# Attention block: causal mask products ahead of the score products in the second block's banks

## The chip, the cores and the metric

The kernel runs on one core of a Trainium2 chip. The metric is the device time of one execution in microseconds; the time before is 558.08 us, the median of three runs (558.05 to 559.54).

## The reference, cut to what matters

Sixteen sequences of 256 tokens, width 128, go through layer norm and causal attention with 16 heads (query and key width 8, value width 64), then through layer norm and a mixture of 8 experts. The change is in the causal scores:

```python
scores = jnp.einsum('bhqd,bhkd->bhqk', q, k) / scale
causal = jnp.triu(jnp.ones((T, T), dtype=bool), k=1)
scores = jnp.where(causal, -jnp.inf, scores)
attn = jax.nn.softmax(scores, axis=-1)
```

## The kernel before, in words

The work of the attention is cut into 64 units (`UNITS = B * G`): one sequence of 16, and one group of 4 heads of 16. The 256 queries of a unit are two blocks. Queries 0 to 127 see keys 0 to 127 only; their scores for 4 heads fill one PSUM bank, `s0_ps` (128 queries x 4 heads x 128 keys). Queries 128 to 255 see all 256 keys; their scores fill two banks, `s1_ps` (128 queries x 4 heads x 256 keys), heads 0 and 1 in the first bank, heads 2 and 3 in the second. In the trace both tiles are called `s_ps`.

The heads are packed so that one matmul does several. A unit's queries `qT` have 32 rows for each head, and `k_diag` holds the keys of head i in the rows of head i and zeros elsewhere. The scores of the first block are one matmul over all 128 rows (line 1276, 512 columns). Those of the second block are two matmuls over 64 rows each (line 1189): rows 0 to 63 (heads 0, 1) write the first bank, rows 64 to 127 (heads 2, 3) the second. The two use different halves of TensorE's array, so they run side by side.

The causal mask is added by matmuls too. In the second block only keys 128 to 255 need one. It goes in two halves of 64 keys, each for both row halves: four matmuls (line 1194) of a 64 x 128 stationary `half_rows` and a moving `half_masks` of 64 columns, broadcast over two heads (128 columns), all bf16. The operands of line 1189 are of type fp32r (shown as f32 in rows), and each of the two writes all 512 columns of its bank; it begins the sum there (`start=True`), and the masks are added.

```python
tiles = ((slice(0, HALF), 0), (slice(HALF, P), 2))
for rows, i in tiles:
    nc.tensor.matmul(s1_ps[:, i:i + 2, :], qT[kb][rows, q, P:T], k_diag[kb][rows, q, i:i + 2, :], start=True, stop=False, ...)
```

Every matmul of the program is a weight load (LDWEIGHTS, the engine PEld in rows) and a product (MATMUL, PE in rows).

Each engine's order is written out by hand, in a function `batch` for each engine: 20 batches of 4 units, some of them in a hardware loop. In step u TensorE does, in this order: scores and masks of the second block of unit u+1 (the block that the change touches, behind a wait on `exp1`, the count of units whose second block ScalarE has finished reading), eight transposes of the probabilities of unit u-1 (`turn`, lines 1048 and 1049), in one of four steps each the products of the query and key projection, a router product or transposes of a norm, the context of unit u-2 (`contexts`, line 1075), the output projection of unit u-3 (`project`, line 1084), four more transposes (`turn_last`, line 1058), a part of the value projection for a later unit (lines 1034 to 1036), and the first block's scores of unit u+2 (line 1276), behind a wait on `filled0`.

VectorE takes the row maximum of the first block (line 939, after `s0_done`) and of the second (line 883, after `s1_done`), and refills `s0_ps` with the mask (line 892). ScalarE takes the exponentials (line 529), 4 for each block. GpSimd scales the probabilities (lines 482 and 489). The increment of `s1_done` stands on the last matmul of the block that is changed. After unit 63 the experts follow, on TensorE's matmuls too.

Of the kernel before, what the change touches and what calls it, by code (L numbers as in the profile page):

```python
# [13 lines left out]
P = 128  # L14
B, T, D = 16, 256, 128
# [27 lines left out]
def has(index, n):  # L43

    return not isinstance(index, int) or 0 <= index < n


def await_count(engine, sem, count):

    if not isinstance(count, int) or count > 0:  # L50
        engine.wait_ge(sem, count)


def bcast(ap, axis, n):

    ap = ap.unsqueeze(axis)
    shape = list(ap.shape)
    shape[axis] = n
    return ap.broadcast_to(shape)
# [6 lines left out]
def block_kernel(nc, x, w_q, w_k, w_v, w_o, gate_w, w1, w2, out):  # L66
# [3 lines left out]
    with ExitStack() as ctx:  # L70
# [3 lines left out]
        def ps(name, shape):  # L74
            return ctx.enter_context(nc.psum_tensor(name, shape, F32))
# [47 lines left out]
        with ExitStack() as early:  # L123
            def sa(name, shape, dt=F32):
                return sb(name, shape, dt, early)

            k_diag_even = sa("k_diag_even", [P, G, HG, T], F32R)
            k_diag = [k_diag_even, sa("k_diag_odd", [P, G, HG, T], F32R)]
            qT = [sa(f"qT{r}", [P, G, T], F32R) for r in range(RING)]
# [14 lines left out]
            half_rows = sa("half_rows", [P, 2, P], BF16)  # L144
            half_masks = sa("half_masks", [P, 2, HALF], BF16)
# [29 lines left out]
        s1_ps = ps("s1_ps", [P, HG, T])  # L175
# [854 lines left out]
        def _(pe):  # L1030
            pe.wait_ge(consts2, 3)

            def split_product(out_, w_h, w_l, x_h, x_l):
                nc.tensor.matmul(out_, w_h, x_h, start=True, stop=False)  # L1034
                nc.tensor.matmul(out_, w_h, x_l, start=False, stop=False)  # L1035
                return nc.tensor.matmul(out_, w_l, x_h, start=False, stop=True)  # L1036
# [141 lines left out]
            def batch(b, par):  # L1178
                for j in range(G):
                    u = b * G + j  # L1180
                    r1, r2, rm = (j + 1) % RING, j % RING, (j + 1) % RING
                    if has(u + 1, UNITS):
                        q, kb = (j + 1) % G, par if j < 3 else 1 - par
                        if isinstance(u, int) and u == -1:
                            pe.wait_ge(halves, 10)
                        await_count(pe, exp1, u + 1)
                        tiles = ((slice(0, HALF), 0), (slice(HALF, P), 2))
                        for rows, i in tiles:
                            nc.tensor.matmul(s1_ps[:, i:i + 2, :], qT[kb][rows, q, P:T], k_diag[kb][rows, q, i:i + 2, :],  # L1189
                                             start=True, stop=False, skip_group_check=True)  # L1190
                        for half in range(2):
                            cols = slice(P + half * HALF, P + (half + 1) * HALF)
                            for rows, i in tiles:
                                last = nc.tensor.matmul(s1_ps[:, i:i + 2, cols], half_rows[rows, half, :],  # L1194
                                                        bcast(half_masks[rows, half, :], 1, 2),
                                                        start=False, stop=(half == 1), skip_group_check=True)
                        last.then_inc(s1_done, 1)
                    if has(u - 1, UNITS):
                        turn(u - 1, rm)
                    if j == 3 and has(b + 2, B):  # L1200
# [5 lines left out]
                        for w in range(2):  # L1206
                            last = split_product(misc_ps[0][:, w * T:(w + 1) * T], wqk_hi[:, w, :], wqk_lo[:, w, :],
                                                 xT_hi[par][:, :], xT_lo[par][:, :])
# [12 lines left out]
                    if j == 2 and has(b + 2, B):  # L1221
                        pe.wait_ge(xn1_ready, b + 3)
                        await_count(pe, v_ready, u + 2)
                        for tb in range(TB):
                            last = nc.tensor.transpose(misc_ps[0][:, tb * P:(tb + 1) * P], xn1[:, tb, :], ident[:, :])
# [19 lines left out]
                    if has(u + 2, UNITS):  # L1245
                        w, q = u + 2, (j + 2) % G
# [16 lines left out]
                        cols = slice((q // 2) * 512, (q // 2 + 1) * 512)  # L1263
                        split_product(misc_ps[0][:, :], xT_hi[xb][:, toks], xT_lo[xb][:, toks],
                                      wv_hi[:, cols], wv_lo[:, cols]).then_inc(v_done, 1)
                    if has(u + 2, UNITS):

                        q, kb = (j + 2) % G, par if j < 2 else 1 - par
# [5 lines left out]
                        if isinstance(u, int) and u == -2:  # L1274
                            nc.tensor.matmul(s0_ps[:, :, :], ident_bf[:, :], bcast(causal[:, :], 1, HG), start=True, stop=True)
                        nc.tensor.matmul(s0_ps[:, :, :], qT[kb][:, q, 0:P], k_diag[kb][:, q, :, 0:P], start=False, stop=True,  # L1276
                                         skip_group_check=True).then_inc(s0_done, 1)

            batches(pe, batch)
            turn(63, 1)  # L1280
            gather(2)
# [92 lines left out]
```

## Time and profile before

| | us |
|---|---|
| median of three runs | 558.08 |
| the profiled execution's own time | 557.51 |
| its span, first to last instruction | 555.8 |
| TensorE (PE) busy in the span | 525.8 |
| VectorE busy | 416.0 |
| ScalarE busy | 405.1 |
| GpSimd busy | 253.6 |
| all 128 matmuls of line 1189 (mean 0.50 each) | 64 pairs |
| all 256 matmuls of line 1194 (median 0.226 each) | 64 times four |

A matmul's row gives its start and a duration that holds its load's rest, its columns and its way through the array; consecutive matmuls overlap, so that the rate at which TensorE works is read from the distance between starts, not from durations. A row "x2" or "x4" in the timeline is several instructions merged: the start of the first, and the time to the end of the last. "64*128 64x512" is a stationary of 64 rows by 128 columns and a moving operand of 64 rows by 512 columns.

### The profile page before, as it was taken

The numbers are of one execution on the slowest core, as the hardware profiler recorded it, in microseconds if no ns is written. First come the engines' busy times: TensorE is split into PE (matmuls) and PEld (weight loads), VectorE is DVE, ScalarE is ACT, GpSimd is POOL, SyncE is SP. The second block draws the span as 40 slices with busy tenths as digits, with TensorE's granted clock in tenths as the row PEclk, the third lists the DMA queues.
The fourth block names the chain that finished last, engine by engine and source line by source line (L and its number), as shares of the span: only waits on it lengthen the run. The fifth ranks groups of instructions, "written<-read, shape, count | busy, mean of one in ns | idle before, by whom it ended". The sixth has DMA issues, their size and how long they took to land.

```text
span 555.8 us, 13959 instructions
## 1 busy us (share of the span) xinstructions
PE 525.8 (95%) x4777; PEld 426.6 (77%) x4777; DVE 416.0 (75%) x1066; ACT 405.1 (73%) x1383; POOL 253.6 (46%) x249
## 2 busy tenths in 40 slices
PE   1489999999999999999999999999999999999996
PEld 1257777777777777778777777777689989999995
DVE  1477888888888888888898998899973876442354
ACT  4699989889888888889889898889655434334330
POOL 5165565565555655565464555457820111011011
PEclk9989999999999999999999999999999999999999
DMA  4577152731633325142250423501200011000011
GB/s 123 151 186 196 39 151 63 243 115 39 173 105 102 90 61 151 38 113 77 77 153 20 133 77 77 140 14 43 92 21 1 2 40 59 20 21 11 11 29 49
DMA packets 49783, 45.97 MB, mean 83 GB/s; under 512 B 4288, under 2 KB 46528, under 8 KB 49728
## 3 DMA queue, kind: packets, MB, share of 16 engines
q1 hardware_dynamic: 48864, 44.60, 29.2%
q8 instruction: 32, 0.52, 0.4%
q10 hardware_dynamic: 864, 0.66, 0.4%
q14 instruction: 23, 0.19, 0.1%
HBM read 26.35 MB, written 18.89 MB: 81 GB/s over the span
## 4 chain that ended last, share of the span: by engine, by line
PE 86%; DVE 5%; ACT 5%; DMA 2%; issue 2%; ACTq 0%; POOL 0%; DVEq 0%
PE ctx_ps L1075 15%; PE misc_ps L1084 11%; PE t_ps L1162 10%; PE t_ps L1048 6%; PE s_ps L1189 5%; PE t_ps L1049 5%; PE t_ps L1058 4%; PE misc_ps L1034 3%; PE s_ps L1146 3%; PE misc_ps L1036 3%; PE misc_ps L1035 3%; ACT prob L529 3%; PE s_ps L1276 2%; PE s_ps L1147 2%; PE s_ps L1148 2%; PE ctx_ps L1172 2%
## 5 line engine op out<-in xcount | busy, mean ns | idle before, releaser
L529 ACT ACTIVATE prob<-s_ps,neg_max 128x128 f32<-128x128 f32 (+1 forms) x512 | 209.6, 436 | 20.6 <-DVE neg_max L939 17.5
L489 POOL TENSOR_TENSOR probn<-prob,inv 128x1024 f32<-128x1024 f32 x64 | 121.2, 1893 | 55.3 <-DVE inv L960 55.3
L529 ACT ACTIVATION_READ_ACCUMULATOR prob<-s_ps,neg_max 128x1 f32 x512 | 113.6, 222 | 0.0
L482 POOL TENSOR_TENSOR probn<-prob,inv 128x512 f32<-128x512 f32 x64 | 66.5, 1040 | 74.6 <-PE t_ps L1058 66.8
L883 DVE TENSOR_REDUCE neg_max<-s_ps 128x4 f32<-128x1024 f32 x64 | 76.3, 1193 | 1.1 <-PE s_ps L1194 1.1
L1084 PE MATMUL misc_ps<-wo_sb,ctxT 128*128 128x128 f32 x512 | 73.9, 287 | 0.7 <-DVE x_all L708 0.7
L506 POOL TENSOR_TENSOR y_parts<-y_sb,y_parts 128x512 fp32r<-128x512 f32 x16 | 20.6, 1286 | 112.9 <-ACT y_parts L587 112.9
L1084 PEld LDWEIGHTS misc_ps<-wo_sb,ctxT 128*128 128x128 f32 x512 | 62.0, 191 | 11.4 <-issue 11.4
L577 ACT ACTIVATE hT<-s_ps 128x512 f32<-128x512 f32 x64 | 38.0, 596 | 44.7 <-PE s_ps L1148 42.2
L1048 PE MATMUL t_ps<-ident,probn 128*128 128x128 f32 x256 | 63.7, 289 | 0.8 <-ACT probT L543 0.7
L1049 PE MATMUL t_ps<-ident,probn 128*128 128x128 f32 x256 | 60.2, 275 | 0.0
L939 DVE TENSOR_REDUCE neg_max<-s_ps 128x4 f32<-128x512 f32 x64 | 44.2, 691 | 16.9 <-PE s_ps L1276 16.4
L753 DVE COPY probT<-t_ps 128x512 f32<-128x512 f32 x64 | 44.1, 689 | 15.7 <-PE t_ps L1058 15.1
L1075 PE MATMUL ctx_ps<-probT,v_odd 128*64 128x256 f32 (+1 forms) x512 | 48.7, 332 | 0.0
L1075 PE MATMUL ctx_ps<-probT,v_even 128*64 128x256 f32 (+1 forms) x512 | 48.7, 332 | 0.0
L747 DVE COPY ctxT<-ctx_ps 128x512 f32<-128x512 f32 x64 | 43.6, 682 | 0.7 <-PE ctx_ps L1075 0.4
L892 DVE CAST s_ps<-causal 128x512 f32<-128x512 bf16 x63 | 42.4, 672 | 0.0
L1075 PEld LDWEIGHTS ctx_ps<-probT,v_odd 128*64 128x64 f32 x512 | 31.7, 136 | 13.9 <-issue 3.6
L1048 PEld LDWEIGHTS t_ps<-ident,probn 128*128 128x128 f32 x256 | 36.1, 141 | 8.0 <-issue 1.3
L1075 PEld LDWEIGHTS ctx_ps<-probT,v_even 128*64 128x64 f32 x512 | 31.7, 136 | 13.6 <-issue 3.2
L543 ACT ACTIVATE probT<-t_ps 128x512 f32<-128x512 f32 x64 | 41.1, 642 | 0.0
L1146 PE MATMUL s_ps<-xin_hi,w_hi 128*128 128x256 f32 x128 | 38.7, 302 | 0.6 <-issue 0.2
(176 smaller groups left out, 1155.2 us busy)
## 6 DMA issues: line engine op xcount, KB each, us to landing
qT<-q_rows SPq DMA_DIRECT2D x15, 512.0 KB, 4.0
q_rows<-qk_hi SPq DMA_DIRECT2D x32, 128.0 KB, 2.4
q_rows<-qk_lo SPq DMA_DIRECT2D x32, 128.0 KB, 2.4
k_diag_odd<-k_rows SPq DMA_DIRECT2D x32, 128.0 KB, 4.2
k_rows<-qk_hi SPq DMA_DIRECT2D x30, 128.0 KB, 2.4
k_rows<-qk_lo SPq DMA_DIRECT2D x30, 128.0 KB, 2.4
k_diag_even<-k_rows SPq DMA_DIRECT2D x28, 128.0 KB, 4.2
w_raw<-in_L_ffn_w SPq DMA_DIRECT2D x1, 2048.0 KB, 9.3
```

What stands on the lines that cost most here:

```text
L482: nc.gpsimd.tensor_tensor(probn[r][:, 0:HG * P].rearrange("p (i k) -> p i k", i=HG), prob[r][:, 0:HG * P].rearrange("p (i k) -> p i k", i=HG),
L489: nc.gpsimd.tensor_tensor(probn[r][:, HG * P:].rearrange("p (i k) -> p i k", i=HG), prob[r][:, HG * P:].rearrange("p (i k) -> p i k", i=HG ...
L529: last = nc.scalar.activation(prob[r][:, first + i * keys:first + (i + 1) * keys], scores[:, i, :], ACT.Exp, bias=neg_max[:, r, block_, i: ...
L753: nc.vector.tensor_copy(probT[rm][:, 1024:1536], t_ps[rm][:, :]).then_inc(t_dve, 1)
L883: nc.vector.tensor_reduce(out=neg_max[:, r1, 1, :], in_=s1_ps[:, :, :], axis=AX.X, op=ALU.max, negate=True).then_inc(max1, 1)
L939: nc.vector.tensor_reduce(out=neg_max[:, r2, 0, :], in_=s0_ps[:, :, :], axis=AX.X, op=ALU.max, negate=True).then_inc(max0, 1)
L1048: nc.tensor.transpose(t[:, i, 0:P], q0[:, 2 * f + i, :], ident[:, :])
L1049: last = nc.tensor.transpose(t[:, i, P:T], q1[:, 2 * f + i, 0:P], ident[:, :])
L1075: last = nc.tensor.matmul(ctx_ps[half * DV:(half + 1) * DV, pair, kb * P:T], v_sb[vb][:, kb, h * DV:(h + 1) * DV], rhs, start=(kb == 0), s ...
L1084: last = nc.tensor.matmul(misc_ps[1][:, tb * D:(tb + 1) * D], ctxT[r][:, c, tb * P:(tb + 1) * P], wo_sb[:, 2 * g + c, :], start=(g == 0 an ...
L1146: nc.tensor.matmul(to, w1_hi[:, e, at_], xh, start=True, stop=False)
L1162: last = nc.tensor.matmul(y_ps[half * CAP:(half + 1) * CAP, q, :], hT[m % RING][:, half, c, q * CAP:(q + 1) * CAP], w2_of(2 * (m % EP) + h ...
```

## The change

The four mask products of the second block go first, and the two score products behind them. The first mask product in each bank carries `start=True`; all the others, the scores among them, add to what is there, or write where nothing of this sum has been written yet. The increment of `s1_done` moves from the last mask product to the second score product. The wait on `exp1` stays ahead of the first of the six. No instruction is added or taken away.

```diff
                         tiles = ((slice(0, HALF), 0), (slice(HALF, P), 2))
-                        for rows, i in tiles:
-                            nc.tensor.matmul(s1_ps[:, i:i + 2, :], qT[kb][rows, q, P:T], k_diag[kb][rows, q, i:i + 2, :],
-                                             start=True, stop=False, skip_group_check=True)
                         for half in range(2):
                             cols = slice(P + half * HALF, P + (half + 1) * HALF)
                             for rows, i in tiles:
-                                last = nc.tensor.matmul(s1_ps[:, i:i + 2, cols], half_rows[rows, half, :],
-                                                        bcast(half_masks[rows, half, :], 1, 2),
-                                                        start=False, stop=(half == 1), skip_group_check=True)
+                                nc.tensor.matmul(s1_ps[:, i:i + 2, cols], half_rows[rows, half, :],
+                                                 bcast(half_masks[rows, half, :], 1, 2),
+                                                 start=(half == 0), stop=False, skip_group_check=True)
+                        for rows, i in tiles:
+                            last = nc.tensor.matmul(s1_ps[:, i:i + 2, :], qT[kb][rows, q, P:T], k_diag[kb][rows, q, i:i + 2, :],
+                                                    start=False, stop=True, skip_group_check=True)
                         last.then_inc(s1_done, 1)
```

TensorE's order in a unit of the steady part, between the first block's scores and the transposes (`k_diag_odd` is the key tile of one of two sequences in flight, `probn` the scaled probabilities):

```order
 L1276 MATMUL s_ps<-k_diag_odd,qT 128x512 [waits filled0]
-L1189 MATMUL s_ps<-k_diag_odd,qT 128x512 [waits exp1]
-L1189 MATMUL s_ps<-k_diag_odd,qT 128x512
-L1194 MATMUL s_ps<-half_masks,half_rows 128x2x64 x4
+L1191 MATMUL s_ps<-half_masks,half_rows 128x2x64 [waits exp1]
+L1191 MATMUL s_ps<-half_masks,half_rows 128x2x64 x3
+L1195 MATMUL s_ps<-k_diag_odd,qT 128x512 x2
 L1048 MATMUL t_ps<-ident,probn 128x128 [waits t_act,normed]
 L1049 MATMUL t_ps<-ident,probn 128x128
```

The wait on `exp1` now stands on the first mask product; what comes ahead of the six and behind them is the same. The first unit of all, at the program's start, where the scores of the first block follow on a bf16 product (line 1275), and the query and key projection follows:

```order
 L1275 MATMUL s_ps<-causal,ident_bf 128x512 [waits first_loaded]
 L1276 MATMUL s_ps<-k_diag_even,qT 128x512
-L1189 MATMUL s_ps<-k_diag_even,qT 128x512 [waits halves]
-L1189 MATMUL s_ps<-k_diag_even,qT 128x512
-L1194 MATMUL s_ps<-half_masks,half_rows 128x2x64 x4
+L1191 MATMUL s_ps<-half_masks,half_rows 128x2x64 [waits halves]
+L1191 MATMUL s_ps<-half_masks,half_rows 128x2x64 x3
+L1195 MATMUL s_ps<-k_diag_even,qT 128x512 x2
 L1034 MATMUL misc_ps<-xT_hi,wqk_hi 128x256 [waits v_ready,xT_ready]
```

The wait on `halves` (the mask constants) moved with the first of the six. The orders of the other engines are the same before and after.

## Rows read from the trace of the kernel before

**Rows 1.** The page, part 1: busy time of each engine
```profile
PE 525.8 (95%) x4777; PEld 426.6 (77%) x4777; DVE 416.0 (75%) x1066; ACT 405.1 (73%) x1383; POOL 253.6 (46%) x249
```
**Rows 2.** Busy time, three stretches: us, then PE, PEld, DVE, ACT, POOL, clock, DMA
```profile
42.60:366.20 323.60, 323.54 (x2732) 251.60 (x2732) 279.75 (x704) 286.95 (x1094) 184.50 (x163) 1.00 0.38 104
366.20:398.00 31.80, 30.40 (x260) 23.60 (x260) 30.14 (x76) 28.48 (x99) 22.13 (x17) 1.00 0.19 59
398.00:555.80 157.80, 151.32 (x1688) 137.94 (x1686) 85.33 (x234) 60.18 (x105) 28.25 (x25) 1.00 0.08 23
```
**Rows 3.** Chain that ended last, in order of time, where it enters and leaves TensorE
```profile
40.78 1.83 ACT prob L529 x8
42.62 0.04 issue
42.66 0.50 PE s_ps L1189
...
366.25 1.48 PE ctx_ps L1075 x16
367.73 0.04 issue
```
**Rows 4.** Line 1189 from 42.6 to 365: count, ns min/median/max, idle before
```profile
L1189 PE MATMUL s_ps<-k_diag_odd,qT x56: 491/500/504, 42.7 to 341.2; 64*128 64x512 f32 x56
L1189 PE MATMUL s_ps<-k_diag_even,qT x56: 491/500/501, 65.5 to 364.6; 64*128 64x512 f32 x56
  ACT prob L529: 0.9, 2
```
**Rows 5.** Timeline of PE in one unit: start us, us, instruction
```profile
204.36 0.60 PE L1058 MATMUL t_ps<-ident,probn 128*128 128x128 f32 x4
204.72 0.48 PE L1034 MATMUL misc_ps<-wv_hi,xT_hi 128*128 128x512 f32 x1
205.03 0.39 PE L1035 MATMUL misc_ps<-wv_lo,xT_hi 128*128 128x512 f32 x1
205.26 0.39 PE L1036 MATMUL misc_ps<-wv_hi,xT_lo 128*128 128x512 f32 x1
205.50 0.40 PE L1276 MATMUL s_ps<-k_diag_even,qT 128*128 128x512 f32 x1
205.82 0.50 PE L1189 MATMUL s_ps<-k_diag_even,qT 64*128 64x512 f32 x2
206.17 0.29 PE L1194 MATMUL s_ps<-half_masks,half_rows 64*128 64x128 bf16 x4
206.38 0.33 PE L1048 MATMUL t_ps<-ident,probn 128*128 128x128 f32 x1
```
**Rows 6.** The same, windows begun late: the last of line 1058, the last two of line 1194
```profile
204.69 0.27 PE L1058 MATMUL t_ps<-ident,probn 128*128 128x128 f32 x1
206.23 0.22 PE L1194 MATMUL s_ps<-half_masks,half_rows 64*128 64x128 bf16 x2
```
**Rows 7.** Timeline of the weight loads (PEld) in the same unit
```profile
205.04 0.19 PEld L1036 LDWEIGHTS misc_ps<-wv_hi,xT_lo 128*128 128x128 f32 x1
205.82 0.19 PEld L1189 LDWEIGHTS s_ps<-k_diag_even,qT 64*128 64x128 f32 x2 [0.36 <-issue]
206.16 0.12 PEld L1194 LDWEIGHTS s_ps<-half_masks,half_rows 64*128 64x128 bf16 x4 [0.16 <-issue]
```
**Rows 8.** Timeline of PE and PEld at the first unit, clock at half
```profile
22.68 0.65 PE L1275 MATMUL s_ps<-causal,ident_bf 128*128 128x512 bf16 x1
22.77 0.98 PE L1276 MATMUL s_ps<-k_diag_even,qT 128*128 128x512 f32 x1
22.68 0.36 PEld L1276 LDWEIGHTS s_ps<-k_diag_even,qT 128*128 128x128 f32 x1
```
**Rows 9.** Timeline of ACT and DVE around the same unit as rows 5
```profile
204.85 0.26 ACT L529 ACTIVATION_READ_ACCUMULATOR prob<-s_ps,neg_max 128x1 f32 x1
205.93 0.69 DVE L939 TENSOR_REDUCE neg_max<-s_ps 128x4 f32<-128x512 f32 x1 [0.24 <-PE s_ps L1276]
206.62 1.19 DVE L883 TENSOR_REDUCE neg_max<-s_ps 128x4 f32<-128x1024 f32 x1
204.95 0.66 ACT L543 ACTIVATE probT<-t_ps 128x512 f32<-128x512 f32 x1
```

## Prediction

> **What bounds the kernel now.** I read the page's busy times first: TensorE is busy for 525.8 us of the 555.8 us span, every other engine for 75% or less [rows 1]. By stage this is sharper. From 42.6 to 366.2 us, the steady part of the attention, TensorE is busy 323.54 of 323.60 us at full granted clock, with VectorE at 279.75 and ScalarE at 286.95 [rows 2]. The chain that ended last says the same: it enters TensorE at 42.66 us with a product of line 1189, and runs on that engine alone until the context products that begin at 366.25 us [rows 3]. From there to 398 us the chain goes through VectorE and ScalarE (30.14 and 28.48 us busy of 31.80), and from 398 us on TensorE leads again [rows 2]. So in the steady part what shortens TensorE's stream shortens the kernel, one for one, and what shortens it after 366 us does not, or in part.
>
> The block of six matmuls that is reordered stands 64 times in the program. In the steady part line 1189 has 56 + 56 matmuls, two to a block, so 56 blocks [rows 4].
>
> Then the timeline of TensorE within one unit, by distances between starts [rows 5, 6]:
> - scores, line 1189, start at 205.82; masks, line 1194, at 206.17: 0.35 us
> - first pair of masks at 206.17, second pair at 206.23: 0.06 us
> - second pair of masks at 206.23, transposes, line 1048, at 206.38: 0.15 us
>
> The block takes 206.38 - 205.82 = 0.56 us. The same three distances stand in all the steady blocks that I looked at, to 0.01 us.
>
> What makes up the 0.35 us? Two products of 512 columns that follow each other in full height (all 128 rows) start 205.50 - 205.26 = 0.24 us apart (0.23 for the two before) [rows 5]. There the next weight load starts 0.01 us after the product ahead of it and is done in its shadow (205.04 against 205.03) [rows 5, 7]. At line 1189 the load and the product start together, at 205.82: the array had just changed from one tile of 128 rows to two of 64, and nothing hides this load [rows 5, 7]. So 0.35 - 0.23 = 0.12 us of the block is a bare load of fp32r weights. The last transpose of line 1058 gives 0.11: it starts at 204.69, line 1034 needs a load of the same size behind it, and line 1035 starts at 205.03, 0.34 later, which is 0.11 for the load and 0.23 for the product [rows 5, 6]. Starts are rounded to 0.01, so I split the 0.41 us from the scores to the second masks as 0.34 + 0.07 (it reads 0.35 + 0.06); the whole block, 0.56, stays.
>
> **The change, part by part.** Nothing is added or removed; the six matmuls and their six loads stay. Their order changes what each load can hide behind.
>
> 1. *Change into the 64-row tiles.* Line 1276 to the block: 205.82 - 205.50 = 0.32 us [rows 5]. It is 0.09 more than 0.23, the array running empty. It is still there, now ahead of a mask product. Taken as unchanged: 0.
>
> 2. *First to second pair of masks.* 0.07 us, taken over from the split above. The first pair's own load was as bare before as it is now: in the old order the mask loads too started only at 206.16, when the scores' columns were through [rows 7].
>
> 3. *Second pair of masks to the scores.* This pair of kinds (bf16, 128 columns, then an fp32r load on the same 64 rows) is not in the trace. The near row is line 1058 to line 1034, 128 columns and then an fp32r load in full height: the load takes 0.11 us from the start of the product ahead, the product's 0.05 us of columns lie inside it [rows 5, 6]. Bounds: from below 0.06 us, if the load were wholly hidden (then the masks' own columns set it); from above 0.17 us, if the load starts when the columns are through (0.06 + 0.11). I take 0.11. For it speaks also the first unit of all: there the fp32r load of line 1276 starts in the same hundredth as the bf16 product of line 1275 (22.68 us), and line 1276 is there 0.09 us later, long before the 0.65 us of that product are over [rows 8]. So a bf16 product does not keep back an fp32r load behind it.
>
> 4. *Scores to the transposes.* Now the 512 columns stand last in the 64-row tiles, with a change back to full height behind them. The same in the other direction is line 1276 to line 1189, 0.32 us [rows 5]. The other way to it: masks to transposes take 0.15 now for 0.05 of columns, so 0.10 for the change of tiles; 0.10 + 0.23 = 0.33. I take 0.32 to 0.33.
>
> The new block: 0.07 + 0.11 + 0.33 = 0.51 us. The old one: 0.56 us. **Gain 0.05 us for each block**, 56 x 0.05 = 2.8 us.
>
> In words: 0.11 us of bare load at the front are traded for a load that is half hidden by the second pair of masks.
>
> The eight blocks outside: the first four (23 to 38 us) stand where ScalarE or the clock sets the pace, the last four where the chain is VectorE's and ScalarE's [rows 2, 3]. I cost them at nothing; all eight at the full rate would be 0.4 us.
>
> *Waits.* The wait on `exp1` stands ahead of the six as before. Behind it on TensorE stands everything else, so I looked at how far it is from holding: ScalarE's last step on the unit before ends at 204.85 + 0.26 = 205.11, and the block starts at 205.82, 0.71 us later [rows 5, 9]. In the whole steady part ScalarE held this line for 0.9 us, twice, at the very start [rows 4]. The transposes of line 1048 wait for ScalarE's copy, which ends at 204.95 + 0.66 = 205.61 against 206.38: 0.77 us to spare [rows 5, 9]. A block shorter by 0.05 us uses up none of this, since each unit's ScalarE work begins with a TensorE product that now comes earlier by as much. VectorE needs 279.75 us for what would take 320.8 instead of 323.6, ScalarE 286.95 [rows 2]. *The increment of `s1_done`* is now on the second score product. It would come some 0.05 us earlier than before; and VectorE's line 883 starts at 206.62, when its own line 939 is over, not when the increment comes [rows 9]. Worth nothing, and costs nothing.
>
> *SP's and GpSimd's queues* issue in the same order; the loads of `qT` and `k_diag` wait on `s1_done` of a sequence before, and that moves with the rest.
>
> Sum against the profiled execution: 557.51 - 2.8 = 554.7 us. The median of the runs shown is 0.57 us above this execution: 558.08 - 2.8 = **555.3 us**, 0.5% less than before. About 0.3% (1.7 us) is what a measurement of this kernel can tell from no change.
>
> **A rule weighed against it.** The four mask loads of a block lie within 0.12 us, and the second pair's products start 0.06 us after the first's [rows 5 to 7], so a load on 64 rows can lie under a product on the same 64 rows. But the mask loads behind the scores did not: they start 0.34 us after them [rows 7]. The Trainium skill (TensorE: Matmul & The Clock Gate, Part 3) says that a weight load overlaps with products in flight only when their row groups differ. By that rule the scores' load would wait out the second masks. The skill's Part 2 allows a load into a background weight buffer as well, which is what the mask rows look like. The rule as a mechanism is the first rival.
>
> **The rivals.**
> - *The load waits for the masks' columns: no difference.* Step 3 is 0.17 instead of 0.11 us: the block is 0.07 + 0.17 + 0.33 = 0.57 against 0.56, the time 558.1 (with half a hundredth either way, 557.8 to 558.4). For it: between line 1189 and line 1194, the only change of kind inside the 64-row tiles, the load was not hidden [rows 7]. Against it: the load behind line 1275 was, and the second mask loads are [rows 7, 8]. Chance 0.20.
> - *Slower: a bf16 product on 64 rows must drain before an fp32r load on the same rows begins*, as at a change of tiles. Place: between the second masks and the scores, in every unit. Price: 0.15 (masks to what follows a drain) + 0.11 (bare load) = 0.26 in step 3, the block 0.07 + 0.26 + 0.33 = 0.66, 0.10 longer; 56 x 0.10 = 5.6 us, 563.7 us. It decides from step 3 above 0.16 us, where the gain is gone. For it only that the load behind line 1189 was late; against it that it was late by no more than the columns, and not by a drain. Chance 0.05.
> - *More than forecast.* The scores' load is hidden wholly (step 3 = 0.06), or the change of tiles behind fp32r costs less than I took. The block is 0.46 us, the gain 56 x 0.10 = 5.6 us, 552.5 us. For it nothing in the rows but the loads that are grouped tightly; against it that one load at a time lies ahead of the running product everywhere else. Chance 0.06.
> - *TensorE's gain is lost to a wait on ScalarE or VectorE:* it needs the 0.7 us to spare to go; it counts to the no-difference case, with 0.02 of its own.
>
> **How the numbers follow.** Forecast 0.67, no difference 0.20 + 0.02, slower 0.05, more 0.06. The forecast's own range is a gain of 0.035 to 0.07 us a block (steps 3 and 4 each off by a hundredth or so), 2.0 to 3.9 us, 554.2 to 556.1 us. The range must also take in no difference: 554.0 to 558.4 us; outside it stand the slower case, the large gain and a little of each side. Faster by over 0.3% (below 556.4): 0.67 + 0.06 = 0.73. Slower: 0.05. Within: 0.22.
>
> **What would show each step right or wrong.** In the timeline of the changed kernel: masks first, the second pair 0.07 us after the first; the scores' load starts with the second pair and not 0.05 us behind it; the transposes start 0.51 us after the first mask (0.57: no difference; 0.66: slower). Units of the steady part lie 0.05 us closer, and the context products at which the chain leaves TensorE begin at about 363.5 us instead of 366.25 us. The forecast is wrong if the start of the transposes is 0.55 us or more behind the first mask, or if waits for ScalarE appear ahead of the masks.

## The result and the profile after

The changed kernel takes 555.28 us (median of 4 runs, 554.97 to 555.69), the kernel before 558.28 us (the three runs shown ahead and one more). The ratio is 0.9945, 95% interval 0.9933 to 0.9957: 3.0 us less. In a later series on one chip the changed kernel took 554.18 us against 558.23 us, ratio 0.9931 (0.9909 to 0.9954). Forecast were 555.3 us and a gain of 2.8 us.

The profiled execution took 555.17 us, with a span of 553.4 us. First the page's part 1, which answers to [rows 1]:

```profile
PE 524.4 (95%) x4777; PEld 424.7 (77%) x4777; DVE 415.9 (75%) x1066; ACT 405.9 (73%) x1383; POOL 253.9 (46%) x249
```

The same stretches as [rows 2], in the changed kernel's times (us, then PE, PEld, DVE, ACT, POOL, clock, DMA):

```profile
43.30:363.96 320.66, 320.63 (x2730) 249.31 (x2730) 279.37 (x704) 287.32 (x1092) 184.52 (x163) 1.00 0.38 104
363.96:396.00 32.04, 30.45 (x260) 23.55 (x260) 30.35 (x76) 28.61 (x100) 22.28 (x17) 1.00 0.18 59
396.00:553.40 157.40, 151.09 (x1687) 137.73 (x1685) 85.19 (x234) 60.22 (x105) 28.19 (x25) 0.99 0.08 23
```

The steady part is still all TensorE's, and it is 320.66 us long where it was 323.60: the gain is in the stage where it was looked for. The two stages behind it kept their lengths to 0.4 us, and the start, ahead of it, is 0.70 us longer.

TensorE's busy time over the whole span fell by only 1.4 us (525.8 to 524.4), and a reader who had only that would miss half of the gain. In the steady part it fell by 2.91 us (323.54 to 320.63). Ahead of it, it rose by 1.7 us, and there the two profiled executions differ in the granted clock, 0.96 before and 0.88 after:

```profile
0.00:42.60 42.60, 20.55 (x103) 13.44 (x103) 20.79 (x55) 29.47 (x89) 18.73 (x46) 0.96 0.58 156
0.00:43.30 43.30, 22.26 (x103) 14.09 (x103) 21.03 (x55) 29.72 (x89) 18.88 (x46) 0.88 0.63 167
```

The chain that ended last, where it enters and leaves TensorE, as in [rows 3] (start us, us, what):

```profile
41.44 1.83 ACT prob L529 x8
43.28 0.05 issue
43.32 0.28 PE s_ps L1191 x4
...
364.05 1.48 PE ctx_ps L1075 x16
365.53 0.04 issue
```

It enters 0.66 us later than before and leaves 2.20 us earlier. The later entry is no effect of the order: in a second profile of the same code (below), with a granted clock of 0.96 in the start, the unit that starts here at 49.51 us starts at 48.62 us, and before it started at 48.87 us.

The timeline of PE in the same unit as [rows 5], and the second pair of masks from a window begun late, as in [rows 6]:

```profile
204.48 0.39 PE L1036 MATMUL misc_ps<-wv_hi,xT_lo 128*128 128x512 f32 x1
204.71 0.40 PE L1276 MATMUL s_ps<-k_diag_even,qT 128*128 128x512 f32 x1
205.04 0.28 PE L1191 MATMUL s_ps<-half_masks,half_rows 64*128 64x128 bf16 x4
205.14 0.48 PE L1195 MATMUL s_ps<-k_diag_even,qT 64*128 64x512 f32 x2
205.55 0.33 PE L1048 MATMUL t_ps<-ident,probn 128*128 128x128 f32 x1
...
205.11 0.22 PE L1191 MATMUL s_ps<-half_masks,half_rows 64*128 64x128 bf16 x2
```

And the weight loads of the block, which answer to [rows 7]:

```profile
205.04 0.11 PEld L1191 LDWEIGHTS s_ps<-half_masks,half_rows 64*128 64x128 bf16 x4 [0.36 <-issue]
205.11 0.19 PEld L1195 LDWEIGHTS s_ps<-k_diag_even,qT 64*128 64x128 f32 x2
205.54 0.14 PEld L1048 LDWEIGHTS t_ps<-ident,probn 128*128 128x128 f32 x1 [0.24 <-POOL probn L482]
```

Line 1276 to the block is 0.33 us (0.32 before). From the first masks to the second 0.07 us, from there to the transposes 0.44 us: the block is 205.55 - 205.04 = 0.51 us, and was 0.56. The scores' load starts at 205.11, in the same hundredth as the second pair of masks. And every block is alike: line 1195 from 42.6 to 365 us has this row for one of its two key tiles (count, ns min/median/max), and no idle time of TensorE ahead of it:

```profile
L1195 PE MATMUL s_ps<-k_diag_odd,qT x56: 477/477/478, 43.4 to 339.3; 64*128 64x512 f32 x56
```

The score products last 477 ns each, against 500 [rows 4], and start later within the block; these durations alone would tell only half of the gain.

A measure that is free of the start and the end of the program is the distance between the sixth of the 64 blocks and the sixty-first, 55 units. Before, from 48.87 to 370.09 us, it is 321.22 us; after, from 49.51 to 367.89 us, 318.38 us. That is **0.052 us less per unit**. The experiments are read by it, since a single execution's time also holds the start, which varied by up to 1.2 us between these profiles, and the end, which varied by more.

### The profile page after: what moved, and what is told of

It reads as the page before. It is cut to its first block, busy times and chain, and to the rows that moved or that the text cites. A ratio compares the mean times of both kernels' runs of the same rounds, so it can differ in the third digit from the quotient of the medians.

```text
span 553.4 us, 13959 instructions
## 1 busy us (share of the span) xinstructions
PE 524.4 (95%) x4777; PEld 424.7 (77%) x4777; DVE 415.9 (75%) x1066; ACT 405.9 (73%) x1383; POOL 253.9 (46%) x249
## 4 chain that ended last, share of the span: by engine, by line
PE 86%; DVE 6%; ACT 4%; DMA 2%; issue 2%; ACTq 0%; POOL 0%; DVEq 0%
PE ctx_ps L1075 15%; PE misc_ps L1084 12%; PE t_ps L1162 10%; PE t_ps L1048 6%; PE t_ps L1049 5%; PE t_ps L1058 5%; PE misc_ps L1034 3%; PE s_ps L1146 3%; PE misc_ps L1036 3%; PE misc_ps L1035 3%; PE s_ps L1195 3%; ACT prob L529 3%; PE s_ps L1276 3%; PE s_ps L1147 2%; PE s_ps L1148 2%; PE s_ps L1191 2%
```

## The experiments

The edits below are shown against the changed kernel and shortened; where a fence has words in place of code, it sums the edit up.

The theory: TensorE sets the pace, and the block costs its columns, its changes of tiles, and of each load what no running product covers. Before, the fp32r load of the scores (0.11 us) stood bare behind the change of tiles; now a bf16 load stands there, which costs almost nothing bare, and the fp32r load lies half under the second masks. Rivals: the load isn't covered at all and the gain is from elsewhere; only what stands last in the block counts; the masks ahead of the scores are free.

### The scores between the two halves of the masks

```diff
-masks 0, masks 1, scores
+masks 0 (start=True), scores, masks 1 (stop=True, then_inc)
```

> The first pair of masks, then the scores, then the second pair. Theory (each load costs what the product ahead of it does not cover; an fp32r load takes 0.11 us and starts with the product ahead, a mask load behind scores waits until their columns are through): the scores' load starts with the first masks and their columns 0.12 to 0.13 us after the block's start; the second masks start at about 0.36 us, the transposes at 0.52 us (changed kernel 0.51, kernel before 0.56). Rival (what counts is only which kind stands last ahead of the full-height transposes, masks 0.56 or scores 0.51): 0.56 us. Rival (the load is not covered by masks at all, the gain is from elsewhere): 0.56 us or more.

Timeline of PE in one block:

```profile
205.81 0.23 PE L1191 MATMUL s_ps<-half_masks,half_rows 64*128 64x128 bf16 x2
205.85 0.48 PE L1196 MATMUL s_ps<-k_diag_even,qT 64*128 64x512 f32 x2
206.17 0.23 PE L1191 MATMUL s_ps<-half_masks,half_rows 64*128 64x128 bf16 x2
206.33 0.33 PE L1048 MATMUL t_ps<-ident,probn 128*128 128x128 f32 x1
```

The second masks start 0.36 us and the transposes 0.52 us after the block's start, as the sum of steps gives. The 55 units take 369.12 - 49.83 = 319.29 us, 0.017 us a unit more than the changed kernel. What stands last does not decide: masks are last here, and the block is 0.52 and not 0.56 us. One execution took 555.91 us, the kernel before beside it 557.26 us.

### A wider mask product over the load

```diff
-cols = slice(P + half * HALF, P + (half + 1) * HALF)
+cols = slice(P, P + HALF) if half == 0 else slice(P, T)
...
```

> The second pair of masks is widened from 128 to 256 columns (it adds zeros to the first 64 keys of each head, so nothing is left out). Theory: the scores' load of 0.11 us begins with the second pair and is covered by whichever is longer, so 0.05 us more columns cost nothing or 0.01 us: the transposes start 0.51 to 0.52 us after the first mask, and the time stays within 0.5 us of the changed kernel. Rival (the load starts only when the masks' columns are through, or the columns set the step): 0.56 us and 3 us more than the changed kernel.

```profile
204.92 0.23 PE L1194 MATMUL s_ps<-half_masks,half_rows 64*128 64x128 bf16 x2
204.99 0.27 PE L1194 MATMUL s_ps<-causal_halves,half_rows 64*128 64x256 bf16 x2
205.02 0.48 PE L1198 MATMUL s_ps<-k_diag_even,qT 64*128 64x512 f32 x2
205.43 0.33 PE L1050 MATMUL t_ps<-ident,probn 128*128 128x128 f32 x1
204.99 0.19 PEld L1198 LDWEIGHTS s_ps<-k_diag_even,qT 64*128 64x128 f32 x2
```

The second pair has twice the columns (its own duration rises from 0.22 to 0.27 us), its first half zeros that GpSimd writes once. The scores' load (PEld) again starts with that pair, and the transposes still start 0.51 us after the first masks. The scores' own row starts 0.03 us behind the wide pair, long before its 256 columns are through (0.12 us, as half of the 0.23 us that 512 take): the row of an fp32r product behind a bf16 product does not tell when its columns begin, so the block is read by the start of the transposes. The 55 units take 367.77 - 49.39 = 318.38 us, to the hundredth what they take in the changed kernel; the execution took 554.75 us. So in the changed kernel some 0.05 us of every block is TensorE waiting for the scores' load, and columns put there cost nothing. This is the sharpest test of the theory: the columns of the masks do not set that step, the load does.

### The scores in two steps

```diff
-scores of two heads, 512 columns
+scores of one head, 256 columns; then of the other, 256 columns, with their own loads
```

> Masks first as in the changed kernel, and each score product of 512 columns cut in two of 256 with a load of its own. Theory (an fp32r load is hidden under an fp32r product in the 64-row tiles as in full height, where 256-column products start 0.12 us apart): the second pair of score products has its load covered, the block is about 0.52 us (two steps of 0.12 for one of 0.23). Rival (in the 64-row tiles nothing is loaded behind fp32r columns, as the mask loads of the kernel before): 0.11 more, 0.62 us, and 6 us more than the changed kernel. This tells whether the late mask loads of the kernel before were late for their kind or for the tiles.

```profile
205.05 0.28 PE L1191 MATMUL s_ps<-half_masks,half_rows 64*128 64x128 bf16 x4
205.15 0.48 PE L1196 MATMUL s_ps<-k_diag_even,qT 64*128 64x256 f32 x4
205.56 0.33 PE L1048 MATMUL t_ps<-ident,probn 128*128 128x128 f32 x1
205.23 0.19 PEld L1196 LDWEIGHTS s_ps<-k_diag_even,qT 64*128 64x128 f32 x2
```

The last row is of the second pair of score loads alone: they start at 205.23 us, while the first pair of products, begun at 205.15, runs. Two more loads in each block, and it is 0.51 us; 367.91 - 49.51 = 318.40 us for the 55 units, 555.10 us for the execution. An fp32r load does hide under fp32r columns on the same 64 rows. The rival, that nothing is loaded behind fp32r columns in the 64-row tiles, falls.

### No masks

```diff
-the four mask products
+scores with start=True
```

> The mask products of the second block are left out (the output lacks the causal mask there), the scores begin the sum. Theory: a bare load of 0.11, 0.23 for the columns and 0.10 for the change of tiles, 0.44 us; so the masks cost 0.07 us a block in the changed kernel and 0.12 in the kernel before. 56 x 0.07 = 3.9 us less than the changed kernel, 551 us. Rival (the masks lie wholly under other work in the changed kernel): 0.51 us and 555 us.

```profile
203.34 0.50 PE L1189 MATMUL s_ps<-k_diag_even,qT 64*128 64x512 f32 x2
203.78 0.33 PE L1048 MATMUL t_ps<-ident,probn 128*128 128x128 f32 x1
```

This kernel leaves the mask out, so its output differs. The block is 0.44 us and begins with a bare fp32r load. In the changed kernel it is also 0.44 us from the start of the scores' load to the transposes (205.11 to 205.55). The 55 units take 364.20 - 49.81 = 314.39 us, 0.073 us a unit less than the changed kernel. All four masks thus cost 0.07 us where they stand now and cost 0.56 - 0.44 = 0.12 us where they stood. The execution took 552.17 us, a microsecond above what was expected; the start was 0.3 us longer than in the changed kernel's profile, and the end behind that unit 0.7 us. That the scores' row lasts 0.50 us again, as before the change, shows the bare load in it.

### A third pair of masks

```diff
-for half in range(2):
+for half in (0, 1, 1):
```

> The changed kernel with the second pair of masks issued twice (its mask is added twice, nothing is left out): six mask and two score products. Theory (TensorE's stream goes into the time one for one; a further bf16 pair ahead of the scores has 0.05 us of columns, and its load hides under the pair ahead): the transposes start 0.56 to 0.57 us after the first mask, 56 x 0.055 = 3.1 us more than the changed kernel, about 558 us, which is the kernel before again. Rival (masks ahead of the scores cost nothing, as they lie under the scores' load): 0.51 us and 555 us.

```profile
206.36 0.34 PE L1191 MATMUL s_ps<-half_masks,half_rows 64*128 64x128 bf16 x6
206.51 0.47 PE L1195 MATMUL s_ps<-k_diag_even,qT 64*128 64x512 f32 x2
206.92 0.33 PE L1048 MATMUL t_ps<-ident,probn 128*128 128x128 f32 x1
```

The block is 0.56 us, and the 55 units take 370.81 - 49.21 = 321.60 us, 0.059 us a unit more than the changed kernel. The execution took 559.45 us, 1.4 us above what was expected, of which 1.4 us lie behind the sixty-first block (557.7 - 370.81 = 186.9 us against 185.5). A further bf16 pair costs its 128 columns (a quarter of the 0.23 us that 512 take) and no load.

Five kernels (no masks, changed, scores between, before, third pair) have blocks of 0.44, 0.51, 0.52, 0.56 and 0.56 us, and 55 units take 314.39, 318.38, 319.29, 321.22 and 321.60 us. What the block loses or gains, the unit loses or gains, to within 0.01 us: TensorE's stream alone decides the length of a unit, from 0.07 us below the changed kernel to 0.06 us above it.

### A bf16 load behind an fp32r product, in full height

Why did the mask loads not hide behind the scores before? The last question was put where no tiles are changed, behind the value projection.

```diff
-nc.vector.tensor_copy(s0_ps[:, :, :], bcast(causal[:, :], 1, HG)).then_inc(filled0, 1)
+nc.tensor.matmul(s0_ps[:, :, :], ident_bf[:, :], bcast(causal[:, :], 1, HG), start=True, stop=True)   # TensorE, every unit
...
```

TensorE now waits for `exp0` itself ahead of that product.

> The changed kernel, and the mask of the first block comes from a bf16 product in full height in every unit (512 columns) instead of VectorE's copy. It asks whether a bf16 load hides behind an fp32r product when no tiles are changed. Theory (it is the kind of load, not the tiles): the load of the bf16 weights starts only with its product, about 0.23 us after the fp32r product ahead of it, while the fp32r load behind the bf16 product starts with that product; each unit is 0.21 to 0.24 us longer on TensorE, 56 x 0.23 = 13 us, 568 us. Rival (only the 64-row tiles hold back a load): the bf16 load starts 0.01 us after the fp32r product ahead of it, as the fp32r loads do; the time differs by less than 1 us from that.

PE and then PEld, where line 1034 is the fp32r product, 1272 the bf16 one and 1273 the scores of the first block:

```profile
211.06 0.40 PE L1034 MATMUL misc_ps<-wv_hi,xT_lo 128*128 128x512 f32 x1
211.30 0.39 PE L1272 MATMUL s_ps<-causal,ident_bf 128*128 128x512 bf16 x1
211.34 0.59 PE L1273 MATMUL s_ps<-k_diag_even,qT 128*128 128x512 f32 x1
...
210.84 0.19 PEld L1034 LDWEIGHTS misc_ps<-wv_hi,xT_lo 128*128 128x128 f32 x1
211.30 0.10 PEld L1272 LDWEIGHTS s_ps<-causal,ident_bf 128*128 128x128 bf16 x1 [0.27 <-issue]
211.30 0.20 PEld L1273 LDWEIGHTS s_ps<-k_diag_even,qT 128*128 128x128 f32 x1
```

The bf16 load starts with its own product at 211.30, 0.24 us after the fp32r product ahead; the fp32r load behind it starts at once. The wait on `exp0` does not explain the late load: ScalarE's last step on the first block before it ended at 208.39 us, 2.9 us earlier, and the load of line 1276 in the kernel before lies under the product ahead although it stands behind a wait too (on `filled0`). The 55 units take 380.98 - 50.11 = 330.87 us, 0.227 us a unit more than the changed kernel, which is what 512 columns take and leaves nothing for an uncovered fp32r load. The time was 568.24 us, the 568 us expected. So it is the pair of kinds, bf16 behind fp32r, and not the 64-row tiles.

### A version that beats both?

The block stands between two changes of tiles, and the context products of line 1075 between two more. Put side by side, one change could go. Three attempts, none a gain.

```diff
 e5_adjoin: scores of the second block; then
+contexts(w, g, vb, r2)
 turn(u - 1, rm), the step's projection or norm products
-contexts(w, g, vb, r2)
```

> The changed kernel, and the context products (tiles of 128 rows x 64 columns) moved from behind the transposes to directly behind the scores (tiles of 64 rows x 128 columns). Per unit the array now changes its tiles three times instead of four. Theory (each change of tiles costs about 0.10 us of empty array, and TensorE's stream sets the pace): 0.10 us less per unit, 56 x 0.10 = 5.6 us less than the changed kernel, about 549.7 us, ratio to the kernel before near 0.985. Rival (ScalarE and VectorE get the transposes 1.45 us later, and their 0.7 us to spare do not cover it): waits ahead of the masks or of the last four transposes, no gain or slower, 555 to 562 us. Rival (a change from row tiles to column tiles drains twice): 555 us.

569.04 us, ratio 1.0204 (1.0175 to 1.0232): slower, by about 2%. Some of the waits in the stretch 60 to 360 us (us in total, times, longest):

```profile
PEld s_ps L1191 <- ACT prob L529: 22.1, 39, 0.7
ACT qk_hi L604 <- PE misc_ps L1036: 18.3, 12, 1.6
ACT xT_hi L600 <- PE misc_ps L1229: 11.9, 13, 1.0
PE s_ps L1191 <- ACT prob L529: 6.1, 25, 0.2
```

ScalarE waits for products that now come behind the contexts, and then TensorE waits at the masks for ScalarE's exponentials. Here TensorE is no longer the bound: it is busy 287.49 of these 300 us, and all 300.00 in the changed kernel. Its own stream behaved as hoped: the timeline has the scores and then the contexts 0.41 us apart, as scores and transposes are in the changed kernel (205.14 to 205.55), so a change from row tiles to column tiles costs no more than one to full height.

```profile
207.07 0.48 PE L1195 MATMUL s_ps<-k_diag_odd,qT 64*128 64x512 f32 x2
207.48 1.52 PE L1075 MATMUL ctx_ps<-probT,v_odd 128*64 128x256 f32 x16
```

The second attempt moves the block down to the contexts:

```diff
-the masks and scores of the second block
 turn(u - 1, rm), the step's projection or norm products
+the masks and scores of the second block
 contexts(w, g, vb, r2)
```

> The changed kernel, and the block of masks and scores moved down, from ahead of the transposes to directly ahead of the context products (behind the query and key projection, router or norm products). As with e5_adjoin the array changes its tiles three times a unit instead of four, but ScalarE and VectorE get the transposes and the projection earlier and not later; only the second block's scores come later, by 0.9 us in most steps and 1.6 us in one of four. Theory (0.10 us per change of tiles, and the delay stays within what ScalarE's loop has to spare): 5 us less than the changed kernel, about 550 us. Rival (ScalarE's exponentials of the second block start right after its copy, 1.0 us behind VectorE's maximum, and the later scores use that up): waits of ScalarE for VectorE's line 883 and of TensorE for ScalarE, 555 us or more, up to 570.

572.62 us, ratio 1.0259 (1.0235 to 1.0283). Again some of the waits from 60 to 360 us:

```profile
DVE neg_max L883 <- PE s_ps L1224: 46.3, 50, 1.6
ACT prob L529 <- DVE neg_max L939: 19.4, 37, 1.0
```

VectorE stands waiting for the late scores in 50 units, 0.93 us on the mean and up to 1.6 us, and ScalarE behind it. In the same series the changed kernel ran once more:

> The changed kernel itself, on the same chip as the others of this call: 0.9945 of the kernel before, 555 us; its steady part, first mask at 49.5 to first mask at 362.5 us, 312.9 us long within 0.1 us.

Its 55 units are 366.99 - 48.62 = 318.37 us long, and the 54 to the block at 361.56 us 312.94 us, as expected.

The third attempt gives ScalarE other work in the idle time that the first one showed:

```diff
 e5_adjoin, ScalarE: exps of the first block
+exps of the second block, heads 0 and 1
 copies of the projection and of the transposes
-exps of the second block, heads 0 to 3
+exps of the second block, heads 2 and 3
```

> e5_adjoin, and ScalarE takes the exponentials of heads 0 and 1 of the second block directly after those of the first block, ahead of the copies that wait for TensorE's transposes and projections (it idled 0.88 and 1.56 us there); heads 2 and 3 stay where they were. Theory (TensorE's stream is shorter by a change of tiles in each unit, and e5_adjoin lost it to that idle time of ScalarE alone): waits of TensorE for ScalarE's line of exponentials fall from 28 us in the stretch 60 to 360 us to a few, 550 to 553 us, faster than the changed kernel. Rival (the later transposes hold back another step of the loop, the turned probabilities or the maxima): 556 to 567 us.

566.41 us, ratio 1.0152 (1.0129 to 1.0175); the profiled execution, at 563.36 us, is the fastest of the four. The wait of TensorE for the exponentials is gone. But ScalarE waits longer for VectorE's maxima (18.6 us, where e5_adjoin had 7.5), and the wait of TensorE's loads for the turned probabilities is left (10.4 us, where it had 9.5):

```profile
ACT prob L529 <- DVE neg_max L941: 18.6, 39, 0.9
PEld t_ps L1060 <- ACT probT L539: 10.4, 27, 0.6
```

So the idle time of ScalarE was not the only thing lost, as the rival said. The loop over three engines has no 1.45 us to give. Of all kernels run that compute the reference, the changed kernel and its versions with the wide masks and with the scores in two steps (one execution each, 554.75 and 555.10 us, no difference that can be told) are the fastest.

## Why the prediction was right

**What bounds.** That TensorE leads from 42.6 to 366.2 us and gives every hundredth on is shown by the five kernels above; the eight blocks outside, costed at nothing, gave no gain that can be told: the stretch behind the start of the sixty-first block takes 185.7 us in the profile before (555.8 - 370.09) and 185.5 us after (553.4 - 367.89), while it ranges from 185.1 us (552.1 - 366.99, the changed kernel again) to 186.9 us (the third pair).

**Step 1, change into the 64-row tiles:** 0.32 us before, 0.33 us after in the rows; unchanged, as taken.

**Step 2, first to second masks:** taken 0.07, measured 0.07 us.

**Steps 3 and 4:** taken 0.11 + 0.33 = 0.44, measured 205.55 - 205.11 = 0.44 us. That the 0.11 is the load and not the columns is shown by the wide masks; that the load is not begun later than the second masks is shown by the kernel without masks, whose bare load has the same 0.44 us ahead of the transposes. The value came from line 1058 to line 1034, the near row in another height. It carried over, and three pairs of kinds behaved alike in both heights in these runs: fp32r behind bf16 and fp32r behind fp32r overlap, bf16 behind fp32r does not.

**Sum.** 0.05 us a block forecast, 0.052 us a unit measured; 2.8 us forecast, 2.8 us in the 55 units, 3.0 us between the medians. That the median came to 0.02 us from the 555.3 us forecast is luck: the same kernel's median was 554.18 us in the later series, 4.05 us below the kernel before there, though its 55 units are the same length (318.37 us); what moved the rest is not shown.

**Not right in detail:** the contexts at which the chain leaves TensorE were forecast at 363.5 us and begin at 364.05 us, since the start of that execution was 0.6 us longer, at the lower granted clock shown above. The expected time without masks, 551 us, was off by 1.2 us because its start and its end were longer.

Two readings were wrong and changed nothing. ScalarE did not hold line 1189 twice at the very start of the steady part: one of the two entries is at 42.66 us, the other at its end, at 364.60 us, and that one is 0.36 us, the same idle time of the weight loads as at a change of tiles that nobody holds [rows 7]. And by its own sum the no-difference rival, a block of 0.57 us, is 56 x 0.01 = 0.6 us above the kernel before, 558.6 us and not 558.1.

**The rivals.** "The load waits for the masks' columns" would have given 0.57 us for the block; it is refuted by the row at 205.11 and by the wide masks. The Trainium skill's sentence that a load overlaps only with products on other row groups (TensorE: Matmul & The Clock Gate, Part 3) does not hold for these products: here loads lie under products on the same rows, fp32r under bf16 (both at 205.11 us), fp32r under fp32r (205.23 under 205.15 in the run with two steps) and bf16 under bf16 (the second masks start 0.07 us after the first). "Drain" would have been 0.66 us; there is none. "More than forecast" needed the scores' load to be hidden wholly, and 0.05 us of it is bare still. ScalarE's time to spare was not touched by 0.05 us; the attempts with 1 to 1.5 us used it up.

What stays open: why a bf16 load does not go under fp32r columns. The runs show that it does not, in both heights, and that it costs little; none shows the cause.

## What to carry to other kernels

Behind a change of tiles the first weight load is bare, so let the cheapest load stand first there, and put the dear one behind a product that covers it. What this saves here is the time of the second pair's columns, 0.05 us, which now pass while the scores' load is under way. Read such a change from distances between starts, per repetition and away from the program's ends: four profiles with the same block (the changed kernel twice, wide masks, two steps) agree to 0.03 us in 55 units, under 1 ns a unit, while a busy time over the whole span or a single time also holds what differs in the start and the end. The kernel before has one such profile. And before moving larger pieces to save a change of tiles (about 0.10 us, an estimate from [rows 5, 6]), see what the other engines have to spare: pieces that came 0.9 to 1.6 us later for them cost 11 to 18 us against the changed kernel here.

## What was not expected of the hardware

- A bf16 load never started under fp32r columns, in 64-row tiles (0.34 us after the scores, before the change) or in full height (0.24 us after the product), while fp32r behind bf16, fp32r behind fp32r and bf16 behind bf16 all overlapped.
- It hardly costs anything bare. The mask products of the changed kernel (count, ns min/median/max) last 226 ns where the load is bare (the first pair, 0.23 in the timelines) and 216 ns where it is covered (the second, 0.22):

```profile
L1191 PE MATMUL s_ps<-half_masks,half_rows x256: 216/226/311, 23.6 to 385.8; 64*128 64x128 bf16 x128
```

- Cutting a 512-column fp32r product into two of 256 with a load each cost nothing (318.40 against 318.38 us for 55 units).
